# All per-group stages of a cross-attention and FFN kernel placed anew in the halves of its schedule

## What is computed

```python
def layer(x, context):
    xn = layernorm(x)
    q = xn @ Wq + lora_q(xn)                              # 16 heads of 64
    k, v = (org @ W + lora(org) for W in (Wk, Wv))        # org: the first 124 context tokens
    o = softmax(q k.T / 8) v + softmax(q k_ipa.T / 8) v_ipa   # ipa: the last 4 tokens, own weights
    x = x + o @ Wo + bo + lora_o(o)
    h = bit_linear(layernorm(x), w1)       # activations to 8 bits by row maximum, weights ternary
    h = silu(depthwise_conv_over_tokens(h, conv_w) + conv_b)  # 1024 channels
    return x + bit_linear(h, w2)           # again quantised by the row maximum of h
```

## Time and profile before

| | us |
|---|---|
| median of 3 runs (1667.2 to 1668.99) | 1667.87 |
| the profiled execution | 1667.05 |
| its span in the trace | 1665.0 |
| TensorE busy | 1473.7 |
| VectorE busy | 1278.9 |
| ScalarE busy | 1181.7 |
| GpSimd busy | 728.5 |

### The profile page before, as it was taken

The page is one execution under the profiler, slowest core; times in us unless marked ns, Lnnn a source line. Parts: engine busy times, 40 slices in busy tenths (PEclk is TensorE's granted clock), DMA queues, the critical chain, the costliest instruction groups (busy, mean ns, idle before and its releaser), DMA issues.

```text
span 1665.0 us, 33467 instructions
## 1 busy us (share of the span) xinstructions
PE 1473.7 (89%) x10778; PEld 1189.6 (71%) x10778; DVE 1278.9 (77%) x3029; ACT 1181.7 (71%) x3925; POOL 728.5 (44%) x1085
## 2 busy tenths in 40 slices
PE   7999999989899999989899998989999898988642
PEld 3678777777777777777777777777777777777521
DVE  4263787888878798787878888887878878787876
ACT  2477877858687786968778686867778596877621
POOL 0144445445544445544444544454444445444400
PEclk9999999999999999999999999999999999999855
DMA  7300001000000101000010100000010000000000
GB/s 188 118 28 24 19 15 42 15 27 13 26 28 13 40 13 40 1 26 28 14 39 13 40 13 25 15 26 27 13 40 13 27 13 26 28 1 27 0 13 13
DMA packets 41129, 47.14 MB, mean 28 GB/s; under 512 B 3008, under 2 KB 35200, under 8 KB 41088
## 3 DMA queue, kind: packets, MB, share of 16 engines
q1 hardware_dynamic: 40032, 45.82, 8.9%
q10 hardware_dynamic: 1056, 0.81, 0.2%
HBM read 36.13 MB, written 10.49 MB: 28 GB/s over the span
## 4 chain that ended last, share of the span: by engine, by line
PE 40%; DVE 28%; ACT 20%; issue 11%; DMA 0%; POOL 0%; DVEq 0%; ACTq 0%; POOLq 0%
ACT SM L648 7%; DVE GBS L877 7%; PE PS L460 7%; PE PS L422 6%; PE PS L438 4%; PE PS L521 4%; PE PS L447 4%; PE PS L403 4%; PE PS L473 3%; PE PS L412 3%; DVE GBS L888 2%; ACT H L673 2%; ACT GBS L678 2%; DVE GBS L867 2%; DVE H L895 2%
## 5 line engine op out<-in xcount | busy, mean ns | idle before, releaser
L1030 POOL TENSOR_TENSOR SM<-SM,RC 128x496 f32<-128x496 f32 (+1 forms) x512 | 339.8, 685 | 710.8 <-DVE RC L802 710.8
L648 ACT ACTIVATE SM<-PS,MX 128x124 f32<-128x124 f32 x1024 | 358.8, 365 | 195.7 <-DVE SM L808 193.6
L460 PE MATMUL PS<-KT,QM 128*128 128x128 f32 x2048 | 277.9, 279 | 21.9 <-ACT SM L648 21.8
L460 PEld LDWEIGHTS PS<-KT,QM 128*128 128x128 f32 x2048 | 249.4, 192 | 34.9 <-ACT SM L648 33.7
L1062 POOL TENSOR_TENSOR OTl<-OF,OTh 128x256 fp32r<-128x256 f32 x256 | 216.0, 844 | 5.6 <-ACT OF L642 5.6
L648 ACT ACTIVATION_READ_ACCUMULATOR SM<-PS,MX 128x1 f32 x1024 | 212.3, 207 | 0.0
L447 PE MATMUL PS<-IDF,SM 128*128 128x128 f32 x1024 | 169.0, 288 | 18.8 <-POOL SM L1030 18.7
L640 ACT ACTIVATE OTh<-PS 128x256 fp32r<-128x256 f32 x256 | 99.4, 388 | 108.6 <-PE PS L438 104.7
L806 DVE TENSOR_REDUCE MX<-PS 128x4 f32<-128x496 f32 x256 | 170.2, 665 | 0.0
L438 PE MATMUL PS<-PT,V 128*64 128x128 f32 x2048 | 169.7, 287 | 0.0
L438 PEld LDWEIGHTS PS<-PT,V 128*64 128x64 f32 x2048 | 107.5, 137 | 82.4 <-issue 75.9
(11 more groups left out here) (140 smaller groups left out, 3691.2 us busy)
## 6 DMA issues: line engine op xcount, KB each, us to landing
XIN<-in_x SPq DMA_DIRECT2D x16, 512.0 KB, 3.5
XRES<-in_x SPq DMA_DIRECT2D x16, 512.0 KB, 3.5
out_y<-H SPq DMA_DIRECT2D x16, 512.0 KB, 3.0
CRAW<-in_ctxT SPq DMA_DIRECT2D x16, 256.0 KB, 2.7
RRAW<-in_ctxT SPq DMA_DIRECT2D x32, 128.0 KB, 2.8
QM<-in_Wq SPq DMA_DIRECT2D x1, 1024.0 KB, 10.8
GBS<-in_Wo SPq DMA_DIRECT2D x1, 1024.0 KB, 22.1
k_ipa_columns<-H SPq DMA_DIRECT2D x1, 1024.0 KB, 6.0
```

What stands on the lines that cost most here:

```text
L460: m = mm(psS[:, h, :], QM[:, 2 * q + h // 2, h % 2, TOK * b:TOK * b + TOK], KT[:, 2 * q + h // 2, b, :], start=True, stop=True)
L648: m = act.activation(SM[s % 2][:, h, 0:ORG], psS[:, h, 0:ORG], ACT.Exp, bias=MX[s % 2][:, h:h + 1], accum_out=SU[s % 2][:, h:h + 1])
L1030: m = pool.tensor_tensor(part, part, RC[c % 2][:, 4 * i:4 * i + 4].unsqueeze(2).broadcast_to(shape), ALU.mult)
```

## The change

Every stage's half is set anew. The computation, the number of instructions and their sizes stay.

- The projection units of each quad come in the order Q, K, Q, K, V, V (before Q, K, V, Q, K, V), and `N_Q`, `N_K`, `N_V` are tables with a half for each quad instead of an offset added to the first. `quad_at` takes the table.
- The context is loaded in half 5 (7), split by ScalarE in 7 (8) and by VectorE in 8 as before.
- Residual halves 6 and 7 (4 and 7); `M_POW` 8 (9); normalisation in 9 as before, the maximum behind it in 10 (9), scaling in 11 (10), transposes of the quantised x in 12 (13), broadcast in 14 as before.
- FFN tiles at 15 plus 0, 1, 3, 4, 6, 7, 9, 10 (0, 1, 2, 4, 5, 6, 8, 9). By `M_TILE[-1]` everything behind moves one half: maxima 29 and 30 (28 and 29), their transposes 31, broadcast 33, quantisation 34 to 36, second product 37 and 39, read out in 39 and 41; ScalarE's copy of X2 in 37 (35).
- GpSimd calls `attend` and `attend_low` first in a half instead of last, its image key copies stand with the first V unit, and its bias additions in 17, 19, 21, 23 (16, 18, 20, 22). SyncE's image value loads stand with the first V unit too.

```diff
-U_Q, U_K, U_V = (0, 3), (1, 4), (2, 5)
+U_Q, U_K, U_V = (0, 2), (1, 3), (4, 5)
-N_CIN = 7
-N_CSPLIT = 8
+N_CIN = 5
+N_CSPLIT = (7, 8)
-N_Q, N_K, N_V = (10, 14), (11, 15), (13, 16)
-N_QUAD = (0, 8, 15, 23)
+N_Q = ((10, 17, 24, 31), (12, 20, 27, 34))
+N_K = ((11, 18, 26, 33), (13, 21, 28, 35))
+N_V = ((15, 22, 29, 36), (16, 23, 30, 38))
-M_SCALE = 1
-M_X2 = (4, 7)
+M_X2 = (6, 7)
-M_POW, M_NORM = 9, 9
-M_QT, M_BC1 = 13, 14
+M_POW, M_NORM = 8, 9
+M_ABS, M_SCALE = 10, 11
+M_QT, M_BC1 = 12, 14
-M_TILE = (0, 1, 2, 4, 5, 6, 8, 9)
+M_TILE = (0, 1, 3, 4, 6, 7, 9, 10)
-M_COPY = M_Q2 + 2
+M_COPY = M_Q2 + 3
-def quad_at(n):
-    return N_QUAD.index(n) if n in N_QUAD else None
+def quad_at(n, places):
+    return places.index(n) if n in places else None
...
@@ sync, project
-                q = quad_at(n - N_K[0])
+                q = quad_at(n, N_V[0])
...
@@ tensor, scores
-                        pe.wait_ge(unit_free[0], g.count(UNITS // 2, (u + U_K[1]) // 2 + 1))
-                        pe.wait_ge(unit_free[1], g.count(UNITS // 2, (u + U_Q[1]) // 2 + 1))
+                        pe.wait_ge(unit_free[0], g.count(UNITS // 2, (u + U_Q[1]) // 2 + 1))
+                        pe.wait_ge(unit_free[1], g.count(UNITS // 2, (u + U_K[1]) // 2 + 1))
...
@@ vector, finish
                     normalise(1, XN2, X2).then_inc(ln2_done, 1)
+                if n == M_ABS:
                     dve.wait_ge(ln2_done, g.count(1, 1))
                     dve.tensor_reduce(AR[0][:], XN2, AX.X, ALU.max, apply_absolute_value=True).then_inc(quant[0], 1)
-                if n == M_NORM + M_SCALE:
+                if n == M_SCALE:
...
@@ gpsimd
-                if n in (16, 18, 20, 22) and g.exists():
-                    b = (n - 16) // 2
+                if n in (17, 19, 21, 23) and g.exists():
+                    b = (n - 17) // 2
...
             def steps(g, n):
+                attend(g, n)
+                attend_low(g, n)
                 if g.exists():
                     project(g, n + HALVES)
...
                 residual(g, n)
-                attend(g, n)
-                attend_low(g, n)
```

More of the change, by code:

```diff
@@ L394, in project @@
                 for a in range(2):
-                    q = quad_at(n - N_Q[a])
+                    q = quad_at(n, N_Q[a])
                     if q is not None:
@@ L404, in project @@
                         m.then_inc(unit_full, 1)
-                    q = quad_at(n - N_K[a])
+                    q = quad_at(n, N_K[a])
                     if q is not None:
@@ L413, in project @@
                         m.then_inc(unit_full, 1)
-                    q = quad_at(n - N_V[a])
+                    q = quad_at(n, N_V[a])
                     if q is not None:
@@ L600, in project @@
             def project(g, n):
-                if n == N_CSPLIT:
+                if n == N_CSPLIT[0]:
                     act.wait_ge(c_in, g.count(48, 48))
@@ L610, in project @@
                 for a in range(2):
-                    q = quad_at(n - N_Q[a] - 1)
+                    q = quad_at(n - 1, N_Q[a])
                     if q is not None:
@@ L616, in project @@
                         act.activation(QM[64:128, 2 * q + a, 1, :], psU[u % 2][64:128, :], ACT.Identity).then_inc(unit_free[u % 2], 1)
-                    q = quad_at(n - N_K[a] - 1)
+                    q = quad_at(n - 1, N_K[a])
                     if q is not None:
@@ L622, in project @@
                                        ACT.Identity).then_inc(unit_free[u % 2], 1)
-                q = quad_at(n - N_V[1] - 1)
+                q = quad_at(n - 1, N_V[1])
                 if q is not None:
@@ L780, in project @@
                     normalise(0, XIN, XIN).then_inc(ln1_done, 1)
-                if n == N_CSPLIT:
+                if n == N_CSPLIT[1]:
                     dve.wait_ge(c_high, g.count(1, 1))
@@ L788, in project @@
                         dve.tensor_tensor(XT[1][:, k, :], psU[k], XT[0][:, k, :].bitcast(F32), ALU.subtract).then_inc(unit_free[k], 1)
-                q = quad_at(n - N_V[0] - 1)
+                q = quad_at(n - 1, N_V[0])
                 if q is not None:
@@ L1013, in project @@
                     pool.tensor_tensor(RS[0][:], VE[0][:], HALF[:], ALU.pow).then_inc(ln1_rstd, 1)
-                q = quad_at(n - N_V[0])
+                q = quad_at(n, N_V[0])
                 if q is not None:
```

## The result

The changed kernel takes 1767.24 us (median of four runs, 1762.92 to 1767.59) against 1668.43 for the kernel before beside it: 1.0575 times as long, 95% interval 1.0563 to 1.0588. Its profiled span is 1760.8 us. The forecast was 1736 with a range of 1688 to 1768; the time stands at the range's upper edge, 99 us over the kernel before where 69 were worked out.

The account below looks back on a forecast made before the run. No engine is full; queue order binds, through VectorE's chain from max-reductions to second product. Chain +2.7 and other terms made 4.2 us a group, with clock +0.7 4.9; over 14 groups 69, so 1667 + 69 = 1736 us, range 1688 to 1768.

Parts of the forecast that it names:

- The chain, +2.7: Max-reductions through transposes, broadcast and quantisation to the second product: 28.4 us against 25.7, +2.7 us a group.
- The other terms: Changes in the rest of the group, outside chain and clock: +1.8, -1.2, +0.4, -0.4, +0.7 and +0.2 us.
- the second half of the product: Second product's other half waits for VectorE's read-out, now behind normalisation and first residual: +1.8 us a group, bounds 0.8 and 2.7.
- the first FFN tile: First FFN product loses a K unit ahead of it and waits for the broadcast: +0.7 us a group (0 to 1.0).
- the tiles: Two FFN tile pairs stand in one step without attention between, each waiting 0.8 us: +0.2 a group (0 to 0.8).
- the exponentials' wait: Of the 1.3 us scores waited for exponentials, the smaller part goes as attention of step 5 comes earlier: -0.4 a group.
- The Q unit of half 31: Its bank is freed by the V copy behind the reduction; 1 us, hidden under the wait for the reductions.
- The clock, +0.7: TensorE's clock falls in every group instead of every second: 1.35 us against 0.7, +0.7; +1.4 if also at the transposes.
- the blocks' distance: Sign the forecast is right: max-reduction blocks 99 to 101 us apart in the changed profile.
- Attention flows: Rival, faster: attention no longer held back by VectorE's reductions and GpSimd's products; 1591 us, likelier 1630; chance 0.16.
- The waits overlap: Rival: time lost at the second product is won back behind it; 1.5 to 2 us a group, 1695; chance 0.14.
- The clock stays low longer: Rival: two clock falls a group, each over a product of its own, +3 instead of +0.7: 1768 us; chance 0.06.

Follow-up runs that it names:

- e4: Changed kernel with unread filler products (14 and 34) ahead of the waits for the max-reductions and before the second product: 1718.6 us, ratio 1.0299.
- e12: As e10, but second product in halves 37 and 39 as in the changed kernel, read out behind normalisation and first residual: 1713.61 us, ratio 1.0269.
- e6: Changed kernel with the first half of its second product one half later (38 and 39 for 37 and 39): 1761.4 us, ratio 1.0556.
- e9: Changed kernel with the old FFN tile halves and 16 unread filler products ahead of the wait for the max-reductions: 1643.91 us, ratio 0.9854.
- e7: Kernel before with 16 unread filler products ahead of the wait for the max-reductions: 1658.4 us, ratio 0.9938.
- e10: Changed kernel with broadcast, quantisation and second product one half back; tiles and reductions stay late: 1669.09 us, ratio 1.0003.
- e8: Changed kernel with the old FFN tile halves, moving everything behind the tiles one half back: 1662.01 us, ratio 0.996.
- e2: Kernel before with the new projection unit order and tables alone; FFN halves, context and GpSimd's order as before: 1670.76 us, ratio 1.0006.
- e5: Kernel before with the new FFN halves and GpSimd's attention first, units as before: 1763.29 us, ratio 1.0561.
- e3: Kernel before with the new FFN halves alone (residual, maximum, scale, transposes, tiles, all behind the tiles one half later): 1764.02 us, ratio 1.0564.
- e11: Kernel before with M_HOFF 5 for 4, reductions to second product one half later behind the old tiles: 1764.04 us, ratio 1.0575.

## Why the prediction was right in kind and short in size

**The chain, +2.7: right.** With the clock held up by fillers it is 28.65 us against the 28.4 worked out. Its largest step, the last portion behind attention of step 2, stands in the timeline as written, and the wait before the product is 4.6 us for 4.7. Two of its terms are off and cancel: the second portion, put at 3.65 us, takes 3.4 (872.25 to 875.6), and the last, put at 1.9, takes 2.3 (877.08 to 879.36). Its pair takes 1.61 us and not 1.28, and it runs beside a softmax product of GpSimd (876.51, 1.63 us), as the second pair of the kernel before did (827.76, 1.67 us).

**The other terms: right in sum.** The rest of the group was put at 69.2 + 1.5 = 70.7 us, and is 70.8. Singly: the second half of the product waits 1.7 in the changed kernel, 1.95 alone, for 1.8; the first FFN tile waits 0.6 for the broadcast; the tiles wait 0.8 twice, 1.6 where the earlier trace rows had 1.0, so +0.6 for the +0.2 of the sum; the exponentials' wait went from 1.3 to 0.9. The Q unit of half 31 waits 1.6 for the V copy, under cover of the wait for the reductions as I had put it. 4.2 us a group without the clock were forecast; e4 has 99.4 against 94.9 of a group of the earlier trace rows with the clock up, 4.5.

**The clock, +0.7: the term that failed.** The argument was a fall in every group instead of every second, with 1.4 as the upper bound if the wait at the transposes did it as well. There are two falls in every group but the first, one behind each wait, and each costs 1.5 us: (102.4 - 99.4) / 2. Together 3.0, less the 0.7 of the kernel before: +2.3, above that upper bound too. Where the step went wrong: I knew from the earlier trace rows that a wait of 2.2 us lets the clock fall in every second group, saw that the new order keeps this wait and adds a longer one, and laid the fall on only one of them. Whether a given wait takes a fall could not have been read from its length, as the last section shows. The read-out is a case: its wait takes a fall in e12 and none in the changed kernel.

**Where the 30 us are that were missing** (98.8 measured, 69 forecast). The 14 distances are 88.7 us longer, 20 more than forecast: 1.6 of clock and 0.3 of other terms in each of the twelve middle ones, less 3 in the first and the last. 7 us more lie outside them, where I had put 0 with bounds of 3: the first block comes at 236.14 for 231.98, and the last two blocks are 69.4 us apart for 66.5. The last 3 us are the difference between the medians and the profiled executions.

**Luck in the range.** The forecast's own range, 1702 to 1758 from 2.5 to 6.5 us a group, does not hold the 1767 or the 6.8. Only the stated range does, by 1 us, and its upper edge comes from a rival that was given 0.06. Of the signs named beforehand, the waits, their places and the clock below 1 came out; the blocks' distance, 99 to 101 us, did not.

**The rivals.** "Attention flows" fell: GpSimd's order alone gives 0, and so it does with the new FFN halves. "The waits overlap" was right in one respect that I missed: most of a wait taken away at the product comes back at the transposes (e6), so TensorE waits for VectorE's whole stretch and not for its last portion alone. But it did not lower the change's time to the rival's 1695. "The clock stays low longer" was given 0.06, and its mechanism, two falls a group, each over a product of its own at +3, is nearly what happened: +2.3 for +3. That its 1768 is within 1 us of the time is in part luck, since 10 of the 99 us stand outside its sum.

**What was not expected to be so sharp.** I took the loss for a sum of many moved stages. One half of delay behind the tiles is enough for it: one constant in the kernel before gives the ratio of the whole change, if by a different share of the clock, and one tuple in the changed kernel takes it back. The other moves together are worth -7 us, and some -14 with the clock held up in both kernels (e9 1644, e7 1658).

## What to carry to other kernels

Where every engine works through a fixed order, look at what a moved stage crosses on the engine that ends the chain (here attention of steps 15 and 2, and the normalisation, which came ahead of what TensorE waits for), not at the stage's own length: three such crossings cost 1.7 to 2.0 us a group each. When a wait of TensorE is made or lengthened, ask of each such wait whether the clock falls in it, and price the fall as a term of its own. Compare two kernels only where the clock fell as often in both: e10 looks 7 us slower than e8, and its stages are 1.7 us a group slower. Where a wait can't be taken away, a few products into a free bank keep the clock up: they gave 49 us here in the changed kernel, 11 in the kernel before, 18 in the best one.

## What the runs showed of the hardware

The clock falls on shorter waits than I had thought worth a term, and the wait's length doesn't tell whether it falls. At the wait before the reductions' transposes (L505 or L506) it fell, of 14 groups, in 8 of the kernel before (wait 2.2 us), in 13 of the changed kernel (2.0), in 13 of e2 and 12 of e8 (1.75), but in none of e10 and one of e12, where the wait is 2.0 again and the wait of 1.6 us for the V copy stands ahead of it as in the changed kernel. And the time at the lower level isn't tied to the length of the wait: 3.4 us behind the wait of 4.6 in the changed kernel, but with a wait of 4.4 (e5) the same product and the next step's attention were slow, and a group had 10 us at the lower level. I take this for a part of why e3, e5, e6 and e11, with quite different waits, all end near 1762, but it was only read from their traces. The agreement is closer than costs of stages would make it: in the changed kernel, e3, e5 and e6 nearly all groups are 102.4 us apart to 0.05, with 7, 14, 10 and 10 us at the lower level. Why they meet there is open, and so is what decides between 3.4 us and more; e3, e5, e6 and e11 were not run with their waits filled, so that their time without the clock isn't known.
